# The first layer's aggregate as a three-pass split product, and the softmax row's exponentials in PSUM

## The reference, cut to what matters

```python
def _L0_gnn_ref(X, adj, mask, Wqk, Wv):
    q, k = jnp.split(X @ Wqk, 2, axis=-1)
    v = X @ Wv
    agg = jnp.einsum('bij,bjd->bid', adj, k * mask[:, :, None])
    w = inv_scale * mask * jnp.einsum('bid,bid->bi', q, agg)
    return jax.nn.softmax(w, axis=1)[:, :, None] * v

def _L1_gnn_ref(x, adj, ...):
    query, keyt, value = x @ Wq.T + bq, x @ Wk.T + bk, x @ Wv.T + bv
    weight = adj * jnp.exp(query @ keyt^T)
    return (weight / sum(weight, axis=2)) @ value

x = _layernorm(x + _L0_gnn_ref(x, adj, nodemask, ...), axis=-1)
x = _layernorm(x + _L1_gnn_ref(x, adj, ...), axis=-1)
```

## Time and profile before

| | |
|---|---|
| median of three executions | 315.56 us |
| the profiled execution | 315.87 us |
| its span, first to last instruction | 314.0 us |
| mean granted TensorE clock | 0.994 |
| TensorE busy (matmuls) | 298.9 us, 95% |
| VectorE busy | 222.1 us, 71% |
| ScalarE busy | 197.4 us, 63% |
| GpSimd busy | 142.1 us, 45% |
| the aggregate's matmuls (L553), 128 instructions | 32.9 us |

### The profile page before, as it was taken

One profiled execution on the slowest core, in us unless ns is written; L12 is line 12 of the kernel. 1 busy time (PEld: TensorE's weight loads), 2 busy tenths in 40 slices (PEclk: granted clock), 3 DMA queues, 4 the chain that ended last, 5 costly groups with the idle time before them and its releaser, 6 DMA issues. The chain is left out here.

```text
span 314.0 us, 6528 instructions
## 1 busy us (share of the span) xinstructions
PE 298.9 (95%) x1900; PEld 269.5 (86%) x1900; DVE 222.1 (71%) x689; ACT 197.4 (63%) x456; POOL 142.1 (45%) x178
## 2 busy tenths in 40 slices
PE   8997999999999999999999999999999999999770
PEld 7876999999999999999999999999998999999660
DVE  1375778777777787777778877777788777777652
ACT  3354556677666666676666666766666667665562
POOL 2365554344555544345555444455554444553322
PEclk9999999999999999999999999999999999999997
DMA  7821224232334332233333332224333322110002
GB/s 260 290 70 34 84 87 117 66 106 85 102 117 117 117 117 84 82 87 99 117 117 117 117 94 79 83 96 117 117 117 117 98 81 78 61 53 34 33 35 100
DMA packets 19021, 31.26 MB, mean 100 GB/s; under 512 B 2112, under 2 KB 6336, under 8 KB 19008
## 3 DMA queue, kind: packets, MB, share of 16 engines
q1 hardware_dynamic: 19008, 31.11, 32.1%
HBM read 22.71 MB, written 8.39 MB: 99 GB/s over the span
## 5 line engine op out<-in xcount | busy, mean ns | idle before, releaser
L262 POOL TENSOR_TENSOR rstd<-var_eps,minus_half 128x4 f32<-128x4 f32 x35 | 35.7, 1019 | 152.9 <-DVE var_eps L458 143.4
L322 ACT ACTIVATE x<-x_sum,shift,rstd 128x256 f32<-128x256 f32 x64 | 35.0, 595 | 55.1 <-POOL shift L265 55.1
L536 PE MATMUL ps<-w_hi,xt_hi 128*128 128x512 f32 x128 | 61.7, 482 | 0.5 <-DVE w_lo L523 0.5
L538 PE MATMUL ps<-w_hi,xt_lo 128*128 128x512 f32 x128 | 50.4, 394 | 0.0
L537 PE MATMUL ps<-w_lo,xt_hi 128*128 128x512 f32 x128 | 50.2, 392 | 0.0
L288 POOL TENSOR_TENSOR x1b<-x,bv_all 128x512 f32<-128x512 f32 x32 | 41.3, 1289 | 2.4 <-ACT x L322 2.4
L270 POOL TENSOR_TENSOR xt_lo<-xt_raw,xt_hi 128x512 fp32r<-128x512 f32 x31 | 40.1, 1295 | 4.3 <-ACT xt_hi L316 4.1
L536 PE MATMUL ps<-wv_hi,x1t_hi 128*128 128x258 f32 x128 | 38.8, 303 | 0.0
L322 ACT ACTIVATE x<-x,shift,rstd 128x256 f32<-128x256 f32 x64 | 34.9, 595 | 3.2 <-POOL shift L265 3.2
L538 PE MATMUL ps<-wv_hi,x1t_lo 128*128 128x258 f32 x128 | 36.4, 285 | 0.0
L536 PE MATMUL ps<-x1t_hi,at_hi 128*128 128x256 f32 x128 | 36.3, 284 | 0.1
(11 more groups left out here) (79 smaller groups left out, 649.2 us busy)
## 6 DMA issues: line engine op xcount, KB each, us to landing
xt_raw<-xt_pairs SPq DMA_DIRECT2D x32, 256.0 KB, 2.7
x_raw<-x_pairs SPq DMA_DIRECT2D x32, 256.0 KB, 2.7
out_pairs<-x SPq DMA_DIRECT2D x32, 256.0 KB, 2.1
adjt<-adjt_pairs SPq DMA_DIRECT2D x32, 129.0 KB, 2.1
p<-params SPq DMA_DIRECT2D x1, 770.0 KB, 6.7
p<-params SPq DMA_DIRECT2D x1, 512.0 KB, 3.9
p<-params SPq DMA_DIRECT2D x1, 256.0 KB, 4.3
bv_all<-value_bias SPq DMA_DIRECT2D x1, 128.0 KB, 7.9
```

The costliest lines, as they stand in the source:

```text
L262: nc.gpsimd.tensor_tensor(rstd[r % 2][:, :, :], var_eps[:, :, :], minus_half[:, :, :], ALU.pow)\
L322: last = nc.scalar.activation(out[:, graph(g)], in_[:, graph(g)], ACT.Identity, bias=shift[r % 2][:, layer, g:g + 1], scale=rstd[r % 2][:, ...
L536: nc.tensor.matmul(out, s_hi, m_hi, start=first, stop=False)
L538: return nc.tensor.matmul(out, s_lo, m_hi, start=False, stop=last)
```

## The change

From the fourth pair on (SPLIT = 3) the aggregate is a split product of three passes. ScalarE casts the masked adjacency and x of a pair to their high parts, GpSimd subtracts for the low parts, and TensorE's `aggregate` waits for the low parts and issues six matmuls instead of two fp32 ones. On GpSimd the order of a slot becomes: low part of x, rstd, shift, mask_adj, xt_lo, low part of the adjacency, x1b. On ScalarE the adjacency's cast stands between the layer-0 norm and z, the cast of x at the end of the slot. The row of exponentials is written to PSUM, in the same bank behind the transposed row, and VectorE scales it from there.

```diff
+SPLIT = 3
...
+        x_hi = [sb(f"x_hi{i}", [128, PAIR_X], F32R) for i in range(2)]
+        x_lo = [sb(f"x_lo{i}", [128, PAIR_X], F32R) for i in range(2)]
+        adjm_hi = [sb(f"adjm_hi{i}", [128, PAIR_N], F32R) for i in range(2)]
+        adjm_lo = [sb(f"adjm_lo{i}", [128, PAIR_N], F32R) for i in range(2)]
...
-        exp_row = sb("exp_row", [2, 128])
...
+        def exp_row_ps(r):
+            return yv_ps(r)[0:2, 0, NODES:2 * NODES]
...
+            def low_adjm(u, r):
+                pool.wait_ge(adjm_hi_done, u + 1 - SPLIT)
+                nc.gpsimd.tensor_tensor(adjm_lo[r % 2][:, :], adjm[r % 2][:, :],
+                                        adjm_hi[r % 2][:, :].bitcast(F32), ALU.subtract).then_inc(adjm_lo_done, 1)
+
+            def low_x(u, r):
+                pool.wait_ge(x_hi_done, u + 1 - SPLIT)
+                nc.gpsimd.tensor_tensor(x_lo[r % 2][:, :], x_raw[r % 4][:, :],
+                                        x_hi[r % 2][:, :].bitcast(F32), ALU.subtract).then_inc(x_lo_done, 1)
+
             def slot(t, r):
+                if exists(t + 3) and r + 3 >= SPLIT:
+                    low_x(t + 3, r + 3)
...
+                if exists(t + 3) and r + 3 >= SPLIT:
+                    mask_adj(t + 3, r + 3)
                 if exists(t + 3):
...
+                if exists(t + 3) and r + 3 >= SPLIT:
+                    low_adjm(t + 3, r + 3)
                 if exists(t + 1):
...
-                if exists(t + 3) and r >= 0:
-                    mask_adj(t + 3, r + 3)
...
+            def split_x(u, r):
+
+                act.wait_ge(x_loaded[r % 4], transfers4(u, r))
+                act.wait_ge(agg_done, u - 1)
+                nc.scalar.copy(x_hi[r % 2][:, :], x_raw[r % 4][:, :]).then_inc(x_hi_done, 1)
+
+            def split_adjm(u, r):
+
+                act.wait_ge(adjm_done, u + 1)
+                act.wait_ge(agg_done, u - 1)
+                nc.scalar.copy(adjm_hi[r % 2][:, :], adjm[r % 2][:, :]).then_inc(adjm_hi_done, 1)
...
                     norm(x1[(r + 1) % 2], x1_sum[(r + 1) % 2], 0, r, x1_done)
+                if exists(t + 3) and r + 3 >= SPLIT:
+                    split_adjm(t + 3, r + 3)
...
-                    nc.scalar.activation(exp_row[:, :], w_row_ps(r + 2), ACT.Exp, bias=neg_max[:, 0:1],
+                    nc.scalar.activation(exp_row_ps(r + 2), w_row_ps(r + 2), ACT.Exp, bias=neg_max[:, 0:1],
...
+                if exists(t + 4) and r + 4 >= SPLIT:
+                    split_x(t + 4, r + 4)
...
-                    nc.vector.tensor_scalar(p_row[0:2, :], exp_row[:, :], inv_sum[:, 0:1], None, ALU.mult)\
+                    nc.vector.tensor_scalar(p_row[0:2, :], exp_row_ps(r + 2), inv_sum[:, 0:1], None, ALU.mult)\
...
-                pe.wait_ge(adjm_done, u + 1)
-                pe.wait_ge(x_loaded[r % 4], transfers4(u, r))
+                if r < SPLIT:
+                    pe.wait_ge(adjm_done, u + 1)
+                    pe.wait_ge(x_loaded[r % 4], transfers4(u, r))
+                else:
+                    pe.wait_ge(adjm_lo_done, u + 1 - SPLIT)
+                    pe.wait_ge(x_lo_done, u + 1 - SPLIT)
...
+                    else:
+                        mm = split_product(agg_ps[:, g, :], [(adjm_hi[r % 2][:, n], adjm_lo[r % 2][:, n],
+                                                              x_hi[r % 2][:, graph(g)], x_lo[r % 2][:, graph(g)])])
```

More of the change, by code:

```diff
@@ L141, in build @@
         first_xt_lo_done = sem("first_xt_lo_done")
+        x_hi_done, x_lo_done, adjm_hi_done, adjm_lo_done = sem("x_hi_done"), sem("x_lo_done"), sem("adjm_hi_done"), sem("adjm_lo_done")
         xt_lo_done, adjm_done, x1b_done = sem("xt_lo_done"), sem("adjm_done"), sem("x1b_done")
@@ L552, in aggregate @@
                 for g in range(2):
-                    mm = nc.tensor.matmul(agg_ps[:, g, :], adjm[r % 2][:, graph(g, NODES)], x_raw[r % 4][:, graph(g)],
-                                          start=True, stop=True)
+                    n = graph(g, NODES)
+                    if r < SPLIT:
+                        mm = nc.tensor.matmul(agg_ps[:, g, :], adjm[r % 2][:, n], x_raw[r % 4][:, graph(g)],
+                                              start=True, stop=True)
+                    else:
+                        mm = split_product(agg_ps[:, g, :], [(adjm_hi[r % 2][:, n], adjm_lo[r % 2][:, n],
+                                                              x_hi[r % 2][:, graph(g)], x_lo[r % 2][:, graph(g)])])
                 mm.then_inc(agg_done, 1)
```

## The result

The changed kernel takes 313.28 us, the median of four executions (312.87 to 313.65), against 315.56 before: a ratio of 0.9925 (95% interval 0.9908 to 0.9942). Measured again later on another occasion it took 313.19 us against 315.51, a ratio of 0.9922 (0.9909 to 0.9936). It is 0.75% faster, by about 2.3 us; the forecast was 312.4 us, 3.2 us faster. The profiled execution took 312.87 us with a span of 311.1.

What follows compares the result with a forecast made beforehand. TensorE's own list of matmuls was taken to bound the kernel between fill and drain. Profiled 315.87 - 4.35 (aggregate) + 1.15 (fill) = 312.67 us, so 312.4 us for the median; range 310.9 to 315.6.

Steps and rivals of the forecast that it cites:

- TensorE's list: TensorE's matmuls in steady slots: the six-matmul aggregate saves 0.15 us per pair, 4.35 us over 29; slot 8.79 us, from 8.94.
- The hold on edge: VectorE's edge product beside GpSimd's low part of x: ends at T + 2.07, not T + 1.77, a delay of 0.29 us.
- The first ring: Waits through VectorE to the w transpose: 8.73 us with edge's delay against the list's 8.79, covered by 0.06 us.
- rivals 2 and 3: Edge held for whole overlap, 0.42: 314.4 us, chance 0.15; low x 0.15 later still, ring 9.01: 318.7 us, chance 0.12.
- The second ring: Waits through GpSimd and ScalarE to z and the p transpose: 8.63 us with edge's delay and the new cast.
- The third ring: GpSimd's own round: over at T + 9.02, 0.23 into the next slot, ahead of the x cast it waits for.
- The fill: Slot 0, a chain of waits: x1t_hi 1.24 us later, new cast 0.30, p_row gives back 0.44; +1.15 us taken.
- The row in PSUM: Exponentials in PSUM for VectorE's p_row scaling: costed at nothing in steady slots, gives back up to 0.44 us in the fill.

## Why the prediction was right, and where it was not

- **TensorE's list, right.** 8.79 us per slot were forecast and measured. The sum for 29 pairs was 4.35; the 29 slots give 3.03, and the loop heads hold 1.15 of what is missing (an excess of 0.28, 0.28, 0.30, 0.30, 0.30 against 0.09, 0.07, 0.05, 0.05, 0.05). Of the last 0.17, slot 28 has 0.07 (8.85 us, the slot in which the loop is left); the rest is spread, as the median of the other slots fell by 0.146 and not 0.15. The sum came out right by a part that I had not in it: the six matmuls take 0.80 us and not 0.72, and 0.08 of the saving lies between the x1 transposes and the aggregate, where a term of the prediction had 0.54 us for both kernels.
- **The hold on edge, right to 0.01 us.** It ends at T + 2.08 against T + 2.07. The pattern taken from the cast x1t_hi in the earlier trace rows was the right one of the two, and the run with exp_s in PSUM shows why the other row (the weight product) gave nothing: it has only one SBUF tensor. The rule of the Trainium skill, page SBUF — State Buffer, section "Who interferes with whom", that two SBUF inputs make VectorE contend with a GpSimd read, agrees: 0.69 us against 0.41. It doesn't cover all holds seen here: the cast x1t_hi and the scaling of p_row have one tensor input and were held too, when input and output both lay in SBUF (1.42 us instead of 0.42 in the earlier trace rows, 0.99 instead of 0.27 with the row back in SBUF).
- **The first ring, a term mis-sized.** I added the hold to w's end at T + 5.83. The second weight product ended at T + 5.99 and not at T + 6.12, since at T + 5.83 it had itself been waiting for the projection: in the kernel without the hold it ends at T + 5.70, earlier by about as much as TensorE's list is shorter. So the cover there was not 0.06 but 6.34 - 5.99 - 0.15 = 0.20 us, and rivals 2 and 3 were further off than I gave them.
- **The second ring, right in size and wrongly used.** The p_row was to end 8.79 - 8.48 = 0.31 us ahead of its transpose; it is 0.28 in most slots (0.34 at the loop heads). I asked only whether that was positive. The step that failed is "so TensorE's list still sets the slot": in the first slot of a loop's turn TensorE's sequencer needs some of that lead to get round the loop, and 0.6 us was nearly enough for it. The slots of before contain the hint, 9.03 among 8.94, which I had averaged away. It cost 1.15 us. The sequencer's chain of 0.73 us, shown above, says by how much: what the lead is short of 0.62 us. Measured are 0.28 to 0.30 for 0.33 to 0.36 (changed kernel), 0.05 to 0.17 for 0.53 (three kernels, two of them split, one not) and 0.05 to 0.09 for 0.60 (before).
- **The third ring, a term mis-sized.** The low part of the adjacency was taken at the mask product's 0.61 us and takes 0.73. With it x1b is over at about T + 0.4 and not T + 0.23, and only just ahead of x's low part at T + 0.49.
- **The fill, right in size by a wrong path.** +1.15 was forecast, +0.90 came. I let x1t_hi wait for x's low part because p_row in the earlier trace rows was not let in between two GpSimd instructions. Here it was let in: x1t_hi ended 0.28 us behind x1b, and x's low part had to make room (1.48 us). The price was paid one instruction later, by x1t_lo: its 1.65 us are 0.96 over 0.69. The same product in the kernel that keeps pair 3 as it was, with no low part of x beside it, takes 0.69 us. The 0.96 stand in the norm's start, 6.02 us behind the p transpose of pair 1 in place of 5.06; the new cast ahead of z adds 0.31 (0.30 were forecast), and p_row gives back 0.37, not 0.44: 0.90.
- **The row in PSUM, undersold.** I costed it at nothing in the steady slots. Alone that is so (315.79 us). In the company of the added GpSimd work it is worth 325.04 - 313.28 = 11.8 us, because x1b now stands where p_row is made. The prediction didn't ask what the change would be without it.
- **The sum.** 312.67 for the profiled execution against 312.87. The agreement is better than the terms deserve: that execution started 0.76 us early, by chance; the median, 0.9 us above the forecast, is to 0.2 us the loop heads' 1.15 and the 0.17 of the other slots, less the fill's 0.25.

## What to carry to other kernels

A full engine is shortened by what its list loses, but the cover of every wait in that list shrinks as well, and a wait with 0.3 us of cover is not free where the sequencer has a loop to return: here the cover had to be 0.62 us. Before work is given to GpSimd, list every VectorE instruction beside its new place with its operands: in these runs a product of two SBUF tensors, and a cast or scaling wholly in SBUF, was held to GpSimd's end; with one operand in PSUM it was not, and this kernel had unused PSUM columns for it. And compare the slots of an unrolled loop one by one: a mean hides the one that is about to grow.

## What was not expected of the hardware

- A held VectorE instruction ends a fixed time behind the GpSimd one, 0.12 to 0.19 us less than it takes unheld: 0.08 us for p_row (2x128), 0.29 for edge (128x256, two operands) and for the cast (128x512), 0.54 for x1t_lo (128x512, two operands; its blocker ended at 23.13, it at 23.67).
- The hold seems to work both ways. x's low part, started while x1t_hi was at work, took 1.48 us instead of 1.29, and 1.47 in the second profiled execution.
- TensorE's return of a loop takes 0.73 us from the end of what the last wait of the body waited for to the first matmul of the next turn, and its taken branch 0.21 to 0.23 us of that, the branch not taken 0.08.
- The return of a loop whose body is three times as long cost some 4.4 us once, 2.96 us of it between VectorE's branch and its next instruction, and 1.7 us by the lower granted clock (0.51 at its lowest) that followed on TensorE's idle stretch; the short body cost up to 0.3 us a time. Written out in full the program ran at 8.79 us a slot up to some 225 us and had four longer slots behind that, in which transfers came later.
